# Cross attention and a quantised FFN: preparation folded into the attention program, weights quantised a piece per slot, FFN operands loaded early

## What is computed

```python
# x: (4, 2048, 512) f32, context: (4, 77, 512) f32, 16 heads of 32; FFN inner size 1408
x = x + xattn(layernorm(x), ctx, ctx, Wq, Wo)   # Q, K and V all through Wq, softmax, then Wo
x = x + ffn(layernorm(x))
# xattn: Q = q@Wq.T, K = V = ctx@Wq.T, softmax(Q K^T / sqrt(32)) V, heads joined, @Wo.T
# ffn, each quantiser is fake int8 (scale, round, clip, scale back):
xq = act_quant(x, clip_x)                       # ONE scale from max|x| over the whole tensor
gate, up = xq @ wquant(w_gate).T, xq @ wquant(w_up).T    # wquant: a scale per row
h = act_quant(silu(gate) * up, clip_down)       # again one scale over the whole tensor
return h @ wquant(w_down).T
```

## Time and profile before

| | us |
|---|---|
| median of 3 runs (1254.4 to 1257.57) | 1257.39 |
| the profiled execution, its own time | 1256.07 |
| its span in the trace | 1253.9 |
| TensorE busy (share of the span) | 1148.4 (92%) |
| VectorE busy | 871.8 (70%) |
| ScalarE busy | 683.7 (55%) |
| POOL busy | 120.9 (10%) |
| mean DMA rate | 164 GB/s |

### The profile page before, as it was taken

One profiled execution on the slowest core, in us unless ns is written; L12 is line 12 of the kernel. 1 busy time (PEld: TensorE's weight loads), 2 busy tenths in 40 slices (PEclk: granted clock), 3 DMA queues, 4 the chain that ended last, 5 costly groups with the idle time before them and its releaser, 6 DMA issues. The chain is left out here.

```text
span 1253.9 us, 17607 instructions
## 1 busy us (share of the span) xinstructions
PE 1148.4 (92%) x6508; PEld 651.9 (52%) x6508; DVE 871.8 (70%) x1559; ACT 683.7 (55%) x829; POOL 120.9 (10%) x80
## 2 busy tenths in 40 slices
PE   6457899999999999999999955999999999699898
PEld 4345566666666666666666432444444444244333
DVE  5866577777777777777766553777777777575475
ACT  5744655555555555655554514656666665744440
POOL 0100000000000000000000000000000000165677
PEclk9769999999999999999999977999999999799999
DMA  9841122223222232221112256766777722599977
GB/s 355 323 155 43 51 68 77 91 87 112 76 76 77 81 115 83 86 76 60 51 51 66 70 177 208 250 228 231 243 228 239 246 69 84 232 405 421 418 278 262
DMA packets 112188, 205.37 MB, mean 164 GB/s; under 512 B 40711, under 2 KB 47623, under 8 KB 106095
## 3 DMA queue, kind: packets, MB, share of 16 engines
q1 hardware_dynamic: 112111, 204.34, 46.6%
HBM read 119.02 MB, written 76.90 MB: 156 GB/s over the span
## 5 line engine op out<-in xcount | busy, mean ns | idle before, releaser
L947 PE MATMUL e_G<-e_cT,e_gu 128*128 128x512 bf16 x704 | 182.4, 382 | 27.3 <-DMA e_cT<-e_cb 27.3
L655 PE MATMUL a_Q<-a_xnT,wq 128*128 128x512 f32 x768 | 195.9, 404 | 8.7 <-DVE a_xnT L640 7.7
L920 DVE SCALAR_TENSOR_TENSOR h<-e_U,x_gus,e_sg 128x512 f32<-128x512 f32 x176 | 131.9, 750 | 84.9 <-PE e_U L951 59.1
L869 ACT ACTIVATE e_sg<-e_G,x_gus 128x512 f32<-128x512 f32 x176 | 119.2, 686 | 124.2 <-PE e_G L947 124.2
L655 PEld LDWEIGHTS a_Q<-a_xnT,wq 128*128 128x128 f32 x768 | 140.8, 190 | 86.8 <-issue 58.0
L699 PE MATMUL a_O<-a_wo,a_aT 128*128 128x512 f32 x720 | 183.6, 403 | 0.0
L951 PE MATMUL e_U<-e_cT,e_gu 128*128 128x512 bf16 x704 | 181.7, 381 | 0.0
L1083 PE MATMUL c_Y<-dn,c_cb 128*128 128x512 bf16 x704 | 159.0, 389 | 18.7 <-DVE c_cb L1046 18.7
L699 PEld LDWEIGHTS a_O<-a_wo,a_aT 128*128 128x128 f32 x720 | 130.5, 188 | 46.5 <-issue 19.2
L556 ACT ACTIVATE a_pr<-a_S 77x2048 f32<-77x2048 f32 x64 | 120.2, 1878 | 26.4 <-PE a_S L677 26.4
L947 PEld LDWEIGHTS e_G<-e_cT,e_gu 128*128 128x128 bf16 x704 | 69.1, 98 | 111.5 <-DMA e_cT<-e_cb 27.7
(11 more groups left out here) (135 smaller groups left out, 1306.8 us busy)
## 6 DMA issues: line engine op xcount, KB each, us to landing
x<-x_d SPq DMA_DIRECT2D x32, 1024.0 KB, 7.8
h_d<-h SPq DMA_DIRECT2D x24, 1024.0 KB, 4.1
h<-h_d SPq DMA_DIRECT2D x11, 1536.0 KB, 18.7
a_xr<-in_x SPq DMA_DIRECT2D x64, 256.0 KB, 2.7
x_d<-a_xr SPq DMA_DIRECT2D x64, 256.0 KB, 2.0
out<-c_y SPq DMA_DIRECT2D x15, 1024.0 KB, 11.3
xa<-in_x SPq DMA_DIRECT2D x56, 256.0 KB, 2.7
h<-h_d SPq DMA_DIRECT2D x11, 1280.0 KB, 15.0
```

Source lines behind the costliest of these rows:

```text
L655: mm = nc.tensor.matmul(Q[:], wq[:, wp, j, P * n.g:P * (n.g + 1)], xnT[:, n.par, xp, j], start=(ins == 0), stop=(ins == 3 * KT - 1))
L869: nc.scalar.activation(sg[:, s], G[:, t % GU], ACT.Silu, scale=gus[:, t:t + 1]).then_inc(silued, 1)
L920: nc.vector.scalar_tensor_tensor(out=h[:, place(u, p), t], in0=U[:, t % GU], scalar=gus[:, IT + t:IT + t + 1], in1=sg[:, s], op0=ALU.mult, ...
L947: mm = nc.tensor.matmul(G[:, t % GU], gu[:, k, P * t:P * (t + 1)], cT[:, p, k], start=(k == 0), stop=(k == KT - 1))
```

## The change

`prepare` is gone; `attend` takes over its work, and what the FFN needs from DRAM is loaded while attention runs out.

- Start: SP loads half of Wq, the context, the other half, then x tile by tile into a ring of six (`RINGX`) in place of two blocks of four, then the rest. K is projected ahead of the slots into the four S banks, V of the four batches in slots -5 to -2 behind the transposes. The low part of the context, the low part of Wo and the spreading of K are POOL's.
- The FFN weights go through in pieces of 128 x 512, one per slot from slot 1 on: 22 pieces for gate and up, then for each of the four rows of down three pieces only measured and the same three loaded again and coded (`Step`; 46 steps). Measuring is VectorE's, the code ScalarE's, the cast POOL's, the transpose a DMA's, the store SP's.
- The lags in the slot change (S of item k-2, O of item k-7, `mx` scores of item k+3), and the order on every engine with them; DN now comes before A and has its own semaphore (`summed`).
- In slots 60 to 65 SP loads gate and up, the first two blocks of x1 and the down weight; their places in SBUF are free by then (Q or the transposes are over). Nothing waits for the last stores of x1 at the program's end.
- The partition maxima of both FFN stages are made by broadcast, a TensorE transpose and a VectorE reduce from PSUM, not by POOL. Block 0 of the expansion is cast tile by tile on VectorE, turned by TensorE into a PSUM tensor `T` and copied by ScalarE and VectorE, half each. The other blocks are still turned by DMA.

The core of the diff. In `attend`, SP:

```diff
+                for n in range(TT):
+                    sp.dma_start(xa[:, n], x_t[0, n]).then_inc(xa_in[n], 16)
...
+                def turn_weight(w):
+                    sp.wait_ge(w_cast, w.code + 1)
+                    after(sp, w_out[w.ring], 16 * (w.code // 2), 1 << 30)
+                    sp.dma_start_transpose(wT[:, w.ring, 0:w.width // P], wb[:, w.ring, 0:w.width]).then_inc(w_turned[w.ring], 16)
...
+                    if (n := at(k, 13)) and n.n >= RINGX:
+                        sp.wait_ge(transposed, n.n - RINGX + 1)
+                        sp.dma_start(xa[:, n.n % RINGX], x_t[n.block, n.g]).then_inc(xa_in[n.n % RINGX], 16)
+                    if (w := weight(k - W_FIRST - 3)) and w.coded:
+                        store_weight(w)
+                    if (w := weight(k - W_FIRST - 2)) and w.coded:
+                        turn_weight(w)
+                    if (w := weight(k - W_FIRST)):
+                        load_weight(w)
...
+                    c = k - (STEPS - 4)
+                    if 0 <= c < len(GU_CHUNKS):
+                        sp.wait_ge(q_done, STEPS)
+                        a, z = GU_CHUNKS[c]
+                        for h in range(2):
+                            sp.dma_start(gu[:, IT * h + a:IT * h + z].rearrange("p t k n -> p t (k n)"),
+                                         gu_d[IT * h + a:IT * h + z].rearrange("t p n -> p t n")).then_inc(gu_in[c], 16)
```

POOL:

```diff
+                nc.gpsimd.tensor_tensor(cx[:, 1].rearrange("p k n -> p (k n)"), cx32[:].rearrange("p k n -> p (k n)"),
+                                        cx[:, 0].rearrange("p k n -> p (k n)").bitcast(F32), ALU.subtract).then_inc(cx_lo, 1)
...
+                    if (w := weight(k - W_FIRST - 1)) and w.coded:
+                        pool.wait_ge(w_coded, w.code + 1)
+                        after(pool, w_turned[w.ring], 16 * (w.code // 2), 1 << 30)
+                        nc.gpsimd.tensor_copy(wb[:, w.ring, 0:w.width], wc[:, w.ring, 0:w.width]).then_inc(w_cast, 1)
```

ScalarE, last in the slot:

```diff
+                    if (w := weight(k - W_FIRST - 1)) and w.coded:
+                        act.wait_ge(w_raw_in[w.raw], 16 * (w.i // 2 + 1))
+                        act.wait_ge(w_scaled, w.scale + 1)
+                        after(act, w_cast, w.code - 1)
+                        nc.scalar.activation(wc[:, w.ring, 0:w.width], wraw[:, w.raw, 0:w.width], ACT.Copy,
+                                             scale=winv[:, w.scale:w.scale + 1]).then_inc(w_coded, 1)
```

VectorE, between aT low and mT:

```diff
+                def measure(w):
+                    dve.wait_ge(w_raw_in[w.raw], 16 * (w.i // 2 + 1))
...
+                    nc.vector.tensor_reduce(top, wraw[:, w.raw, 0:w.width], AX.X, ALU.max, apply_absolute_value=True).then_inc(w_measured, 1)
+                    if w.last:
...
+                        own.step(nc.vector.tensor_scalar(sc, wmax[:, col], 1.0 / QMAX, None, ALU.mult))
+                        nc.vector.reciprocal(winv[:, col], sc).then_inc(w_scaled, 1)
...
+                    if (w := weight(k - W_FIRST - 1)) and w.measured:
+                        measure(w)
```

TensorE, ahead of the slots and in them (`W_FIRST` is 1):

```diff
+                            mm = nc.tensor.matmul(S[:, g, 0:NK], wq[:, wp, j, P * g:P * (g + 1)], cx[:, cp, j],
+                                                  start=(ins == 0), stop=(ins == 3 * KT - 1))
...
+                def project_v(b):
+                    if b == 0:
+                        pe.wait_ge(xnT_l, 3)
+                    after(pe, v_rdy, b - 1)
...
+                            mm = nc.tensor.matmul(v_bank(b)[0:KEYS], cx[:, cp, j, KEYS * b:KEYS * (b + 1)], wq[:, wp, j],
+                                                  start=(ins == 0), stop=(ins == 3 * KT - 1))
...
+                    if 0 <= k + 5 < BATCH:
+                        project_v(k + 5)
...
-            return Q if k >= 6 else O if k >= 0 else (O, A, DN)[k % 3]
+            return Q if k >= 7 else O if k >= -4 else (O, A, DN, Q)[k % 4]
```

In `expand`, POOL, VectorE, TensorE and ScalarE:

```diff
-                pool.wait_ge(s_tmax, 1)
-                nc.gpsimd.partition_all_reduce(gmax[:], tmax[:], P, RMAX).then_inc(s_gmax, 1)
+                nc.vector.tensor_copy(tall[:], tmax[:].to_broadcast([P, P])).then_inc(s_tmax, 1)
                 dve.wait_ge(s_gmax, 1)
+                own.step(nc.vector.tensor_reduce(gmax[:], U[:, GU - 1, 0:P], AX.X, ALU.max))
...
+                nc.tensor.transpose(U[:, GU - 1, 0:P], tall[:], id32[:]).then_inc(s_gmax, 1)
+                for t in range(TT):
+                    pe.wait_ge(first_cast, t + 1)
+                    for k in range(KT):
+                        mm = nc.tensor.transpose(T[:, k // 2, TOK * (k % 2) + P * t:TOK * (k % 2) + P * (t + 1)],
+                                                 cb[:, 0, t, P * k:P * (k + 1)], id16[:])
+                    mm.then_inc(first_turned, 1)
...
+                nc.scalar.activation(cT[:, 0, 2:4], T[:, 1].rearrange("p (a n) -> p a n", a=2), ACT.Copy).then_inc(first_rdy, 1)
```

More of the change, by code:

```diff
@@ L463, in attend @@
         FIRST = -12
-        SLOTS = range(FIRST, STEPS + 8)
+        SLOTS = range(FIRST, STEPS + 9)
         def at(k, lag):
@@ L537, in _ @@
                         act.wait_ge(ln_done, done.n + 1)
-                        after(act, att_rdy, done.n)
                         nc.scalar.activation(rcp[:], lnd[:], ACT.Exp, scale=-1.0).then_inc(rcp_rdy, 1)
-                    n = at(k, 8)
-                    for g in (range(TT) if k == -8 else () if not n or k < -4 else (n.g,)):
-                        if g == 0:
-                            act.wait_ge(rs_rdy, n.block + 1)
-                        t = xa[:, n.par, g]
-                        nc.scalar.activation(t, t, ACT.Identity, bias=nb[:, g:g + 1], scale=rs[:, g:g + 1]).then_inc(normed, 1)
+                    now = at(k, -2)
@@ L547, in _ @@
+                    if now:
+                        act.wait_ge(scored, now.n + 1)
+                        after(act, valued, now.n)
+                        nc.scalar.activation(pr[:], S[0:KEYS], ACT.Exp, scale=SM_SCALE).then_inc(exped, 1)
                     if done:
@@ new lines, in _ @@
+                for k in SLOTS:
+                    if k == -8:
+                        pe.wait_ge(id_in, 16)
+                    now = at(k, -2)
+                    if now:
+                        after(pe, maxed, now.n + 5)
+                        after(pe, exped, now.n)
+                        pe.wait_ge(mT_rdy, now.block + 1)
+                        pe.wait_ge(qT_l, now.n + 1)
+                        if now.n == 0:
+                            pe.wait_ge(consts, 2)
+                        if now.n == 0:
+                            pe.wait_ge(k_lo, GROUPS)
+                            pe.wait_ge(v_rdy, BATCH)
+                        for kp, qp in ((0, 0), (0, 1), (1, 0)):
+                            for h in range(HG):
+                                rows = slice(DH * h, DH * (h + 1))
+                                nc.tensor.matmul(S[0:KEYS, h], kt[rows, now.batch, kp, now.g], qT[rows, now.ring, qp],
+                                                 start=(kp + qp == 0), stop=False)
+                        for h in range(HG):
+                            rows = slice(DH * h, DH * (h + 1))
+                            mm = nc.tensor.matmul(S[0:KEYS, h], negw[rows, now.g], mT[rows], start=False, stop=True)
+                        mm.then_inc(scored, 1)
@@ L687, in _ @@
                         mm.then_inc(m_turned, 1)
-                    if (n := at(k, -6)):
+                    if (n := at(k, 3)):
+                        after(pe, exped, n.n - 4)
+                        after(pe, maxed, n.n)
+                        if n.n % PER == 0:
+                            pe.wait_ge(kbd_rdy, HG * (n.batch + 1))
+                            pe.wait_ge(k_lo, GROUPS)
+                        pe.wait_ge(qT_h, n.n + 1)
+                        for t in range(TT):
+                            mm = nc.tensor.matmul(S[:, t, 0:HG * KEYS], qT[:, n.ring, 0, P * t:P * (t + 1)],
+                                                  kbd[:, n.batch % 2, n.g].rearrange("p h k -> p (h k)"), start=True, stop=True)
+                        mm.then_inc(m_scored, 1)
+                    if (n := at(k, -7)):
                         pe.wait_ge(w_split, 2)
```

692 lines of the change are left out of this document (297 added, 395 removed).

## The result

The changed kernel takes 1192.49 us (median of 4 runs, 1190.06 to 1195.00) beside 1257.48 us for the kernel before (4 runs): ratio 0.9481, 95% interval 0.9443 to 0.9519. The profiled execution took 1194.37 us, its span is 1192.5 against 1253.9.

The account below looks back on a forecast made before the run. Preparation was taken as loading and waiting, attention as matmul time on TensorE, with a second hole at the border to the expansion. Terms -40 - 5 + 20 - 14 + 0.5 = -38 us gave 1219 us, range 1194 to 1242.

Parts of the forecast that it names:

- Term 1: Start: S0, the first S matmul of item 0, comes at 71 instead of 110.73; -40 us, S0 bounds 64 and 85.
- Term 2: Drain after the last Q: new order cuts slots from 6.47 to 5.7 us, six slots x 0.8; -5 us, bounds 0 and -8.
- Term 3: Attention slots with weights: VectorE's round grows to 10.6 against TensorE's 9.90 us; +20 us, bounds 0 and +32.
- Rival A: Weight slots: VectorE's loop hides, the added measuring fits into its idle time; 1199 us, chance 0.23.
- Term 4: Border to the expansion: shorter program end, maximum without all-reduce, cast and turn of the last tile only; -14 us, bounds -10 and -15.
- Term 5: Border to the contraction: two small VectorE steps and a transpose replace one POOL instruction; +0.5 us, 0 to 1.2.
- B: Slots lose more: POOL's casts collide with VectorE, or S0 is at 85; 1237 us, chance 0.20.
- C: Weight slots: SP's queue becomes the loop of the slot, each of 46 grows; slower than before, 1288 us, chance 0.05.
- D: Start: V and K interleaved with the first slots hold S0 at 100 or later; 1248 us, chance 0.04.

Follow-up runs that it names:

- e2: Changed kernel with qT low moved ahead of the measuring, the copy of mT and mx on VectorE, from slot 1 on: 1192.43 us.
- e1: Changed kernel with one more reduce on VectorE, its result thrown away, in each of the 34 measuring slots: 1212.38 us.
- e10: Changed kernel with one extra 128x128 matmul within S, between its twelve 32x77 matmuls and its mask, in slots 24 to 59: 1214.14 us.
- e7: Changed kernel with block 0 of the expansion cast by ScalarE in one piece and turned by DMA, as before: 1199.84 us.
- e8: Changed kernel with the partition maximum of the expansion given back to POOL's all-reduce: 1197.98 us.
- e3: Changed kernel with the norm of the next x tile ahead of qT high on ScalarE in the slots before slot 0: 1190.96 us.
- e9: Changed kernel with one extra 128x128 matmul right ahead of Q, which has the same tile shape, in slots 24 to 59: 1200.55 us.
- e5: e3 with the low part of Wo moved from POOL to VectorE in slot -1: 1187.51 us.
- e6: Changed kernel with norm first, Wo's low part on VectorE, xnT low ahead of the small products in slot -1, qT low first from slot 8: 1180.26 us.

## Why the prediction was right and wrong

**Term 1, S0: right in mechanism, 3 us short.** V of batch 0 started at 24.63 (I said 25). S0 came at 73.98 and not 71: the last two Q took 4.58 us each where I had 3.06. Counted from start to start, four V took 12.7 us for my 11.3 (the first, behind 3.26 us of idle time, 4.1), six Q 20.3 for 18.4 and the rest 16.4 for 15.6. TensorE had idled from 56.9 to 59.3, and from 60 to 64 its granted clock is 0.57, so it is mostly at the lower level of 1.2 GHz:

```profile
60.00:64.00 4.00, 4.00 (x13) 3.14 (x12) 0.04 (x1) 0.05 (x1) 1.02 (x1) 0.57 0.00 0
```

One premise was false with no harm: POOL's first sum started at 7.59, right behind its input, and not 9 us into the program like an all-reduce. The sizes I gave for half of Wq and the context are a little low (1.16 and 1.68 MB by their shapes, not 1.13 and 1.64); nothing hung on them.

**Term 2, the drain: right in kind, half in size, and the row agrees by luck.** A slot there takes 5.9 us for 6.47, where I forecast 5.7. The last five items gained 2.7 us (33.3 to 30.6) where I had priced six slots at 0.8. The other 1.9 us of the row's 4.6 lie in the ten items ahead of these, of which nine are shorter by 0.16 to 0.70: not what my term was made of. This rests on the trace alone; no run undid the new order of the drain.

**Term 3, the slots with weights: this failed, twice.** The step "from there to the transposes 0.1, those and the change of shape 0.59 + 0.19 to DN, and from DN's start to the next att 2.40: 10.3 [...] 10.6 against 9.90" has the right round and the wrong length. Measured in the slot above: DN to `att` 2.49, where 2.40 plus 0.3 for the code was taken (the code moved Ln by under 0.1); `att` to the end of qT low 6.79, not 7.0; a hand-over of 0.06, not 0.1; transposes to DN 0.58 with the change of shape in it, where I had 0.59 + 0.19. That is 9.92. The price was 6.3 us by e2 in place of 20 (four full weight slots took 40.4 us and not the 43 of my sum), and e1 shows that there was no slack: another 0.6 costs 0.6. Beside a TensorE slot of 9.90 a round of 9.92 would have cost next to nothing; it has a price only because TensorE's own slot had become shorter, which is the second failure. I had called +20 the likeliest of 0 to +32; for a difference of two sums near 10 us, an error of 0.7 is all of the term.

That is what I held fixed: "TensorE's slot is 9.90 us". I weighed the new order on VectorE alone. On TensorE it removed one change of tile shape in each slot, 0.19 us by e10. That is 8.4 of the 9.95 us that items 4 to 48 win once nothing waits for qT low (e2); less the 6.3 of that wait, term 3 came out at -3.6. Rival A, the loop hides, gives a nearer time (1199) and is refuted by e1: a right number would have come from a wrong reason.

**Term 4, the border: right in sum, -13.8 for -14**, from parts of -2.2 (the program's end: 2.53 to 0.33 of waiting), -5.7 (maximum over partitions) and -5.9 (cast and turn). By e7 the turn undone alone costs 6.1. By e8 the all-reduce undone alone costs 2.7, so it can't be carried elsewhere as 5.7.

**Term 5: right**, +0.3. **Rivals B, C, D**: no cast on POOL held VectorE in the slots (a cast takes 0.61 us; the VectorE instruction that it mostly meets, the low part of xnT, takes 0.69 us with and without it); SP released no wait there; S0 came at 73.98 and not at 100. B's collision is real but elsewhere: at the start, where e3 met it.

## What to carry to other kernels

Where a change moves work into a full loop, sum the round of every engine, also that of the engine which is already the bound, with the order of its tile shapes: a regrouping that saves one change of shape can outweigh what was added. Test slack by doubling the suspected instruction, not by the table of waits. Keep long GpSimd instructions away from VectorE's copies on a critical chain, however small these are.

## What the runs showed of the hardware that I had not expected

- A change of tile shape on TensorE costs 0.19 us and is counted as busy time (e9, e10).
- A VectorE copy of 128x4 took 4.44 us beside a GpSimd sum over 128x2048, and 0.17 without it (e3, e5). At the very start a VectorE sum of 1024 columns took 2.94 us beside the 2.81 of POOL's; the same sum took 1.23 us (at 5.62) before POOL had begun.
- The last two Qs before S0 differ between executions of the same start: 4.58 and 4.58 us in the changed kernel, 5.46 and 4.58 in its second profile, 4.56 and 3.01 in e7. In e5 and e6 both took 2.97 or 2.98. It is not the idle time right ahead of the first that tells these apart (2.40 us in the changed kernel and e7, 3.21 in e5, 2.34 in e6). From 28 to 59 us TensorE was busy for 24.7 us in the changed kernel and for 27.5 and 27.7 in e5 and e6. The cause stays open.
